# A graph network's gathers on GpSimd: one wait per group, until the group before is described

## What is computed

```python
edge_index = jnp.stack([src, dst])
x = _layernorm(x + _L0_gnn_ref(x, edge_index, ...))     # 4 inner layers: MLP on [h[row], h[col]], segment sum by row, MLP on nodes
x = _layernorm(x + _L1_gnn_ref(x, edge_attr_64, edge_attr_9, ..., edge_index))   # attention: q.k per edge, softmax per node, sum of v
x = _layernorm(x + _L2_gnn_ref(x, edge_index, edge_attr_16, ...))                # MLP on [x[src], x[dst], attr], segment sum by dst
x = _layernorm(x + _L3_gnn_ref(x, edge_index))                                   # degree-normalised sum of x[from]
return x
```

## Time and profile before

| | us |
|---|---|
| median of 3 runs | 11431.74 |
| lowest and highest | 11428.04, 11442.52 |
| span of the profiled execution | 14825.9 |
| POOL busy in it (53%) | 7791.1 |
| PE busy (59%) | 8697.7 |
| DVE busy (40%) | 5930.2 |
| ACT busy (15%) | 2258.2 |

### The profile page before, as it was taken

How to read it: one execution, slowest core, us unless ns; L and a number is a source line. 1 busy time by engine, 2 the same in 40 slices (tenths; PEclk the granted TensorE clock), 3 DMA queues, 4 the chain that set the end, 5 groups by cost and what they waited for, 6 DMA issues and landing times. The chain is left out here.

```text
span 14825.9 us, 181348 instructions
## 1 busy us (share of the span) xinstructions
PE 8697.7 (59%) x45043; PEld 7160.7 (48%) x45044; DVE 5930.2 (40%) x14761; ACT 2258.2 (15%) x3991; POOL 7791.1 (53%) x7547
## 2 busy tenths in 40 slices
PE   1003778885555555555655655899994556664332
PEld 0002654443555455445554544688884545554232
DVE  4004750001333333333333333688888823333222
ACT  0000013331000100010001000355551000000000
POOL 4662015555666466646664656355552445554666
PEclk6555557776767666766666667899997867776555
DMA  1001333333111211121111111588884311111111
GB/s 24 1 1 39 108 121 116 115 108 73 39 39 39 61 40 38 39 59 39 39 39 49 39 38 39 156 252 254 253 253 113 104 40 41 43 41 28 22 22 23
DMA packets 853388, 1107.16 MB, mean 75 GB/s; under 512 B 336739, under 2 KB 530568, under 8 KB 852294
## 3 DMA queue, kind: packets, MB, share of 16 engines
q1 hardware_dynamic: 304698, 470.90, 11.0%
q0 software_dynamic: 264160, 418.34, 10.2%
q10 hardware_dynamic: 284332, 215.58, 5.6%
HBM read 896.28 MB, written 207.86 MB: 74 GB/s over the span
## 5 line engine op out<-in xcount | busy, mean ns | idle before, releaser
L1161 POOL DMA_INDIRECT gx_l<-xr,gi_l x4160 | 4264.9, 1025 | 3258.8 <-DVE gi_l L1247 2049.8
L1269 DVE TENSOR_TENSOR aggT_l<-aggT_l,psum 64x128 f32 x4160 | 1160.5, 279 | 3764.2 <-remote 1764.3
L909 POOL DMA_INDIRECT slots_d<-eo,row_d x806 | 785.8, 975 | 1414.7 <-DVE eo L922 902.4
L1792 PE MATMUL psum<-cw,xa 128*128 128x256 f32 x6656 | 1508.9, 381 | 23.0 <-DVE xa L1877 19.6
L1781 POOL DMA_INDIRECT gx<-xr,gi x832 | 920.0, 1106 | 977.4 <-DVEq L1868 629.8
L1792 PEld LDWEIGHTS psum<-cw,xa 128*128 128x128 f32 x6656 | 1232.6, 190 | 237.9 <-issue 86.2
L1323 PE MATMUL psum<-ptab,oht 128*128 x6656 | 1031.3, 311 | 418.6 <-issue 376.7
L1323 PEld LDWEIGHTS psum<-ptab,oht 128*128 128x128 f32 x6656 | 976.1, 228 | 476.9 <-issue 475.8
L1199 PE MATMUL psum<-b,onesb 3*128 3x512 bf16 x520 | 262.6, 505 | 1585.5 <-ACT h_l L1226 1304.5
L2367 POOL DMA_INDIRECT gx_l<-xr,gi_l x832 | 829.0, 996 | 483.3 <-issue 262.9
L1848 ACT COPY xT<-psum 32x512 f32<-32x512 f32 x1664 | 955.9, 574 | 594.4 <-remote 395.0
(11 more groups left out here) (357 smaller groups left out, 13303.7 us busy)
## 6 DMA issues: line engine op xcount, KB each, us to landing
wkv<-slots_d ACTq DMA_DIRECT2D x208, 568.0 KB
kr<-keyrow_s SPq DMA_DIRECT2D x416, 256.0 KB
shb<-shT SPq DMA_DIRECT2D x1664, 64.0 KB
gx_l<-xr,gi_l POOLq DMA_INDIRECT x4992
vtab<-kv ACTq DMA_DIRECT2D x208, 256.0 KB
v_in<-vtab SPq DMA_DIRECT2D x104, 512.0 KB, 3.5
hT<-noderow SPq DMA_DIRECT2D x101, 512.0 KB
kr<-keyrow_d SPq DMA_DIRECT2D x208, 128.0 KB
```

The lines of the kernel that those rows point to most:

```text
L909: e_gone[j].at(pool.indirect_dma_start(slots["d"], bass.IndirectOffsetOnAxis(ap=row["d"][:, c0 + t:c0 + t + 1], axis=0), eo[j][:, t, :], N ...
L1161: pool.indirect_dma_start(gx[j][:, c_, :], None, xr, bass.IndirectOffsetOnAxis(ap=gi[j][:, c_:c_ + 1], axis=0)).then_inc(rows_in[j].sem, 16)
L1269: ins = dve.tensor_tensor(a, a, sums(j, h), ALU.add)
L1792: ins = pe.matmul(bank[2 + p][:, t % 2 * OKV:(t % 2 + 1) * OKV], xa[j][:, c, t * P:(t + 1) * P], cw[:, c, :], start=c == 0, stop=c == KC - 1)
```

## The change

A new semaphore `described` is given to POOL's transfers as `engine_sem`: POOL itself raises it by one when it has described a transfer, while the old semaphore still counts the rows landed. Before the first transfer of a group POOL now waits until the count covers every transfer of the groups before. A group is eight gathers in the edge passes and in the last stage, four in the attention, thirteen scatters by source. The scatters by destination are left alone. The first group of each stage has no such wait. Each new wait has its own no-op behind it, and the loops gain a register operation for the value.

```diff
--- before.py
+++ after.py
@@ -142,6 +142,7 @@
         pe, dve, act, pool, sp = nc.tensor, nc.vector, nc.scalar, nc.gpsimd, nc.sync
         done = sig("dve_step")
         loaded = sig("loaded")
+        described = sig("described")
 
         def join():
             nc.all_engine_barrier()
@@ -892,9 +893,13 @@
                 if c % SC == 0 and c >= 2 * SC:
                     pool.wait_ge(scattered[j].sem, scattered[j].n)
                     pool.nop(nofuse=True)
+                if c and c % SC == 0:
+                    pool.wait_ge(described.sem, described.n)
+                    pool.nop(nofuse=True)
                 scattered[j].at(pool.indirect_dma_start(
                     slots["s"], bass.IndirectOffsetOnAxis(ap=row["s"][:, c:c + 1], axis=0), rec_s[:, c, :], None,
-                    bounds_check=TILES["s"] * P - 1, oob_is_err=False), 16)
+                    bounds_check=TILES["s"] * P - 1, oob_is_err=False, engine_sem=described.sem), 16)
+                described.n += 1
 
         def scatter_d_pool():
             pool.wait_ge(filled_d.sem, filled_d.n)
@@ -1158,7 +1163,11 @@
                             pool.wait_ge(pre_done.sem, pre_done.n + i - (AHEAD - 1))
                         pool.nop(nofuse=True)
                         for c_ in range(W):
-                            pool.indirect_dma_start(gx[j][:, c_, :], None, xr, bass.IndirectOffsetOnAxis(ap=gi[j][:, c_:c_ + 1], axis=0)).then_inc(rows_in[j].sem, 16)
+                            if c_ == 0 and k.has(0, 1):
+                                pool.wait_ge(described.sem, described.n + i * W)
+                                pool.nop(nofuse=True)
+                            pool.indirect_dma_start(gx[j][:, c_, :], None, xr, bass.IndirectOffsetOnAxis(ap=gi[j][:, c_:c_ + 1], axis=0),
+                                                    engine_sem=described.sem).then_inc(rows_in[j].sem, 16)
                 turns(pool, n, depth, lead, turn, AHEAD)
 
             def messages_pe():
@@ -1298,6 +1307,7 @@
             for x in names:
                 sig(x).n += n
             part_added.n += n * (ng - 1)
+            described.n += n * W
             if feature:
                 fe_turned.n += n
                 fe_kept.n += n
@@ -1778,7 +1788,11 @@
                     upto(pool, "gx_read", k, 0, AHEAD)
                     pool.nop(nofuse=True)
                     for t in range(GT):
-                        pool.indirect_dma_start(gx2[r][:, t, :], None, xr2, bass.IndirectOffsetOnAxis(ap=gi1[j][:, t:t + 1], axis=0)).then_inc(rows_in1[r].sem, 16)
+                        if t == 0 and k.has(0, 1):
+                            pool.wait_ge(described.sem, described.n + i * GT)
+                            pool.nop(nofuse=True)
+                        pool.indirect_dma_start(gx2[r][:, t, :], None, xr2, bass.IndirectOffsetOnAxis(ap=gi1[j][:, t:t + 1], axis=0),
+                                                engine_sem=described.sem).then_inc(rows_in1[r].sem, 16)
             turns(pool, G, depth1, lead1, turn, AHEAD)
 
         def logits_pe():
@@ -1920,6 +1934,7 @@
         logits_dve()
         for x in names1:
             s1[x].n += G
+        described.n += G * GT
         for j in range(AHEAD):
             rows_in1[j].n += 16 * GT * (G // AHEAD)
         for j in range(2):
@@ -2364,7 +2379,11 @@
                         pool.wait_ge(summed.sem, summed.n + i - (AHEAD - 1))
                     pool.nop(nofuse=True)
                     for c_ in range(W):
-                        pool.indirect_dma_start(gx[j][:, c_, :], None, xr, bass.IndirectOffsetOnAxis(ap=gi[j][:, c_:c_ + 1], axis=0)).then_inc(rows_in3[j].sem, 16)
+                        if c_ == 0 and k.has(0, 1):
+                            pool.wait_ge(described.sem, described.n + i * W)
+                            pool.nop(nofuse=True)
+                        pool.indirect_dma_start(gx[j][:, c_, :], None, xr, bass.IndirectOffsetOnAxis(ap=gi[j][:, c_:c_ + 1], axis=0),
+                                                engine_sem=described.sem).then_inc(rows_in3[j].sem, 16)
             turns(pool, n3, 4, 6, turn, AHEAD)
 
         def conv_pe():
```

## The result

The change makes the kernel slower: 12,159.0 us median of four runs against 11,432.2, ratio 1.063, interval [1.062, 1.065]. That is 727 us more. I had forecast 11,790 us and a range to 12,360: the sign and the range held, the loss was twice the one forecast.

The account below looks back on a forecast made before the run. POOL, describing transfers nearly back to back, was taken to bound the runs; 679 uncovered waits at 0.52 us add 353 to 11,432, giving 11,785, rounded to 11,790 us, with a range of 11,380 to 12,360.

Parts of the forecast that it names:

- POOL works back to back in the runs: Whole kernel: in plain runs POOL's transfers follow each other nearly without pause, a gather 0.94 us plus 0.30 between.
- the sum of 11,535 us: Whole kernel: stage times added up without late posts, 0.9% above the measured median of the kernel before.
- The late posts belong to the profiled execution: Sorting, edge passes, last stage: PE's posts seen late only under profiling, explaining 14,826 us against 11,432 in runs.
- the recorder: POOL's queue: profile recording taken as the reason PE's posts are seen late; no row shows the records themselves.
- My estimate of 14 transfers: POOL's queue: some 14 transfers until records back up, from about 500 in flight and 264,160 packets for 7436 transfers.
- engine_sem costs nothing: Every counted transfer: POOL's extra post priced at nothing, with 174 us put into the range.
- The attention is covered: Attention: its 207 waits cost nothing, as POOL idles 2.87 us ahead of each group of four; 108 us if uncovered.
- No-op and register operation hidden: Loops: one of each per turn, hidden behind the 0.94 us of the last gather still being described.
- 679 waits on the path at 0.52 us: Passes, last stage, scatters by source: each wait leaves 0.82 us where 0.30 stood, 353 us in all.
- 353 us as the whole cost on the path: Passes, last stage, scatters by source: the only cost added to 11,432, with gathers keeping 0.94 us.
- the bubble is the long one: Rival: first gathers take 1.78 us after each drain, 679 × 1.36 = 923 us more, 12,355 us; chance 0.12.
- late posts: Rival, edge passes and last stage: posts late in runs too, pauses release them, 8.2% faster, 10,490 us; chance 0.17.

Follow-up runs that it names:

- e1: The kernel before, unchanged, run again for a new profile on a chip of the faster kind; run 11,415.0 us, profiled span 11,413.1 us.
- e2: The changed kernel with every transfer still raising the new count but all the new waits removed; 11,426.1 us, ratio 1.000 to the kernel before.
- e4: The changed kernel with each wait asking only for the group before the last; 11,435.0 us, ratio 1.001 to the kernel before.
- e9: The changed kernel with the wait moved ahead of the fifth gather in edge passes and last stage; 11,740.0 us, ratio 1.028 to the kernel before.
- e13: The changed kernel with DVE's one-hot comparisons in passes and last stage cut to one tile of eight; 11,743.2 us, ratio 1.028 to the kernel before.

## Why the prediction was right and where it was wrong

*POOL works back to back in the runs.* Right: e1 has 0.944 us and 0.30 for nearly every transfer, and the sum of 11,535 us was 1% from it. *The late posts belong to the profiled execution*: right that the runs of 11,432 us are free of them, wrong as to why. I left to "the recorder" what plain runs show as well: on three chips those of the kernel before took 14,564 to 14,788 us. My estimate of 14 transfers from the Trainium skill (NOTIFIC — the notification-queue block, "Constraints, capacities, measured rates") explains nothing here: e1 records the same 264,160 packets without a late post.

*engine_sem costs nothing.* Right (e2). *The attention is covered.* Right: its window is 1762 us in e1 and in the change. *No-op and register operation hidden.* Right (e4).

*679 waits on the path at 0.52 us.* The number of waits is right; the gap is 0.45 in the gathers and 0.52 in the scatters, 310 us by the rows and not 353. As the price of the gap this was sized well.

*353 us as the whole cost on the path.* **This is the step that failed.** The sum priced a wait by the gap ahead of it and took every gather behind at its 0.94 us; longer gathers stood in it at nothing, and only the upper end and a rival had them, in the first gather. Measured, the wait costs 1.07 us: 0.45 of gap, and the rest mostly in the second and third gather of the group, with the stalls below. Of two candidates for a first gather, 0.94 and 1.78, I put the 1.78 down to its standing behind an index copy. It was the right row and the wrong reading. DVE goes on behind that copy:

```profile
6036.15 1.22 DVE L1258 TENSOR_TENSOR oh<-node_iota,key_s 128x1024 f32<-128x1024 f32 x1
```

The gather at 6036.40 starts 0.25 us inside the comparison, and ends at 6038.18, 0.8 us after it. The rows I had read could have shown it; I looked at who releases a gather and not at what DVE does while it is described. So the cost was not the bubble alone but also a shift of the later gathers against DVE's work, 372 us net in the passes and the last stage. It doesn't lie in the gather behind the wait, which keeps its 0.94 as I had assumed, but one or two behind it. The rival "the bubble is the long one" had the size nearer (12,355) with the wrong mechanism: e9 pays 0.45 per wait and no more.

*Nothing for stalls.* The 1.86 us gaps, 75 us, were in no term. The attention has gaps of that kind before and after, as POOL idles there; what they are was not tried.

*The rival "late posts".* Its point of decision ("as soon as a turn in the runs is over 10.5 us long") was well put. Where turns are that long the change gains 1.7%, not 8.2%: two thirds of the excess was far too much, since ACT still idles 3725 us for late posts, against 4100 in the kernel before.

The Trainium skill has the rule that I missed (SBUF — State Buffer, "Who interferes with whom"): DVE and GpSimd share one pair of SBUF ports, whole instructions lock it, and an operation with two SBUF inputs contends with GpSimd's reads. The traces agree: gathers that start inside the comparison of two SBUF operands take 1.53 to 1.83 us in the rows shown, while in e1 the 291 that start inside `pre_s`, which reads one operand from PSUM, have a median of 0.944. That page of the Trainium skill infers that such an operation does not stall descriptor generation; for these indirect gathers it does, and the measurement decides.

## What to carry to other kernels

Before pricing a pause on one engine, list what the others do in the stretch behind it: a pause moves the phase between engines, and where two of them exclude each other that can cost as much as the pause. If a wait must stand in a train of transfers, put it where the other engine's colliding work is not due (here the fifth gather instead of the first: 317 us instead of 727), or let it ask for something one group back, which cost nothing.

And when a profile's span and the runs disagree by 30%, the profile isn't of what the runs did: have both taken again on one chip before reading waits from it.

## What was not expected of the hardware

A gather that starts while DVE compares two SBUF operands waits until that comparison is over, and ends 0.82 us after it (median; so do 480 gathers in the change's passes). If the work is four pieces back to back, it gets in behind the first piece in some cases (1.20 us) and behind the last in others (2.24 us).

What happens to a gather that is already under way depends on the operation. The comparison of two SBUF operands doesn't hold it: 101 gathers of e1 see one start in their first 0.5 us, and none takes more than 0.95. The bf16 comparison, which has one SBUF operand and a scalar per partition, does: in the change 447 gathers see one start in their first 0.5 us, and 441 of them last until 0.12 us after it has ended. When it starts later than that, the gather isn't held (491 of e1, median 0.944). This is the 0.21 us of the second gather, and in e13, with that comparison short, it is gone for all but 38 of 454.

The same kernel takes two different times. On three of the seven chips on record, what PE posts while GpSimd describes transfers without a pause is seen up to 20 us late, and this kernel takes 14,564 to 14,788 us instead of 11,425. There the same change is 1.7% faster, and on the others 6.4% slower. Each chip was met at one time only, so chip and moment can't be told apart, and what makes the difference stays open; no kernel could vary it.
